# Routing's one-hot columns: GpSimd multiplies by the token codes, VectorE only compares

## The reference

```
x = x + 0.5 * ffn(layernorm(x))
x = x + attention(layernorm(x))     # 16 heads of 16, causal, 4096 x 4096 scores a head
x = x + 0.5 * ffn(layernorm(x))
```

```
vals, idx = top_k(softmax(x @ gate_w + gate_b, axis=tokens), 2)
y[e] = relu(relu(relu(x @ w1[e]) @ w2[e]) @ w3[e])          # with biases
v[e] = sum over tokens of y[e] * weight of the token for e
out  = sum over the token's two experts of v[e]
```

## Time and profile before

| | |
|---|---|
| median of 3 runs | 2114.99 us (2114.93 to 2117.0) |
| the profiled execution, its own time | 2126.23 us |
| its span | 2124.5 us |
| busy: TensorE / VectorE / ScalarE / GpSimd | 2047.7 / 1817.7 / 1598.6 / 414.5 us |
| mean granted TensorE clock | 0.975 |

### The profile page before, as it was taken

How to read it: one execution, slowest core, us unless ns; L and a number is a source line. 1 busy time by engine, 2 the same in 40 slices (tenths; PEclk the granted TensorE clock), 3 DMA queues, 4 the chain that set the end, 5 groups by cost and what they waited for, 6 DMA issues and landing times.

```text
span 2124.5 us, 99858 instructions
## 1 busy us (share of the span) xinstructions
PE 2047.7 (96%) x43659; PEld 1584.0 (75%) x43659; DVE 1817.7 (86%) x4023; ACT 1598.6 (75%) x3311; POOL 414.5 (20%) x1118
## 2 busy tenths in 40 slices
PE   5899989999999999999999999999999999879998
PEld 3788866377877777777787777777778776658885
DVE  6666666899999999999999999999999994676665
ACT  5344446599999999999999999999999998334442
POOL 1333213411121111121111111111111111023330
PEclk8899989999999999999999999999999999979998
DMA  8211103300010000100001001000010002231112
GB/s 273 74 47 50 42 16 125 134 30 25 13 34 14 25 30 8 34 20 18 31 7 33 22 16 34 9 29 27 11 34 16 22 4 69 54 118 47 45 49 88
DMA packets 70394, 94.36 MB, mean 44 GB/s; under 512 B 16640, under 2 KB 59396, under 8 KB 69956
## 3 DMA queue, kind: packets, MB, share of 16 engines
q1 hardware_dynamic: 62796, 68.75, 10.1%
q0 software_dynamic: 6816, 19.20, 3.4%
q10 hardware_dynamic: 344, 0.01, 0.0%
HBM read 62.24 MB, written 25.43 MB: 41 GB/s over the span
## 4 chain that ended last, share of the span: by engine, by line
PE 88%; DVE 6%; issue 2%; ACT 1%; POOL 1%; DMA 1%; SPq 1%; another core or an unknown queue 0%; DVEq 0%; ACTq 0%; POOLq 0%
PE bank L1264 39%; PE bank L1257 22%; PE bank L1139 17%; PE bank L1346 3%; PE bank L1150 1%; PE bank L1375 1%; DVE stats L1405 1%; PE bank L1307 1%; PE bank L1157 1%; DVE rows L1427 1%; DVE x_res L1725 1%; SPq L698 0%; POOL work L591 0%; DVE work L1594 0%; PE bank L1217 0%
## 5 line engine op out<-in xcount | busy, mean ns | idle before, releaser
L966 ACT ACTIVATE feat<-bank 128x512 f32<-128x512 f32 (+3 forms) x2304 | 1263.2, 565 | 113.8 <-PE bank L1264 13.3
L1264 PE MATMUL bank<-work 96*32 96x512 bf16 (+2 forms) x15872 | 1206.4, 370 | 5.0 <-DVE work L1772 3.8
L1772 DVE TENSOR_REDUCE work<-bank 128x1 f32<-128x512 f32 (+1 forms) x1920 | 1178.9, 659 | 26.4 <-PE bank L1264 23.4
L1257 PE MATMUL bank<-feat,phase 128*17 128x128 f32 (+3 forms) x18432 | 879.2, 263 | 0.3 <-ACT feat L972 0.3
L1257 PEld LDWEIGHTS bank<-feat,phase 128*17 128x17 f32 x18432 | 588.4, 98 | 270.7 <-ACT feat L972 13.7
L1264 PEld LDWEIGHTS bank<-work 96*32 96x32 bf16 (+1 forms) x15872 | 472.6, 96 | 57.1 <-DVE work L1772 24.6
L1139 PE MATMUL bank<-work 128*128 128x256 f32 (+1 forms) x1872 | 398.4, 363 | 0.6 <-issue 0.2
L1139 PEld LDWEIGHTS bank<-work 128*128 128x128 f32 x1872 | 325.1, 192 | 37.1 <-issue 1.0
L625 POOL TENSOR_SCALAR_AFFINE_SELECT feat<-feat 128x128 f32<-128x128 f32 x512 | 145.1, 292 | 456.0 <-ACT feat L966 439.1
L1656 DVE COPY work<-phase 128x514 f32 x234 | 101.5, 436 | 124.1 <-ACT work L880 99.5
L578 POOL DMA_INDIRECT work<-token_table,row_no x142 | 138.1, 973 | 299.0 <-PE bank L1150 142.6
(11 more groups left out here) (201 smaller groups left out, 1371.9 us busy)
## 6 DMA issues: line engine op xcount, KB each, us to landing
phase<-in_w SPq DMA_DIRECT2D x12, 1024.0 KB, 12.0
work<-qk_parts SPq DMA_DIRECT2D x60, 192.0 KB
token_table<-rows SPq DMA_DIRECT2D x8, 1056.0 KB, 8.7
work<-work SPq DMA_DIRECT2D x512, 0.5 KB
qk_parts<-phase SPq DMA_DIRECT2D x20, 384.0 KB, 2.8
work<-qk_parts SPq DMA_DIRECT2D x60, 128.0 KB
qk_parts<-work SPq DMA_DIRECT2D x12, 384.0 KB, 2.8
x_res<-in_x SPq DMA_DIRECT2D x8, 512.0 KB
```

The lines of the kernel that those rows point to most:

```text
L966: eng.activation(p_ring[:, n % P_RING, lo:QB], s_bank("probs", n)[:, lo:QB], ACT.Exp, scale=HD ** -0.5).then_inc(sig.s_done, 1)
L1257: mm = eng.matmul(bank[ACC_BANK][GRID * g:GRID * g + VW, GRID * i0:P], v_aug[:, t, h, :], weights[:, i0:TPJ, g, :], start=(t == 0), stop=( ...
L1264: mm = eng.matmul(out[GRID * g:GRID * (g + 1), width], left[:, GRID * g:GRID * (g + 1)], right, start=start, stop=stop)
L1772: eng.tensor_reduce(maxima[:, h % 2, j, PLACE[i], at:at + 1], scores[:, 0:hi - lo], AX_X, ALU.max).then_inc(sig.a_done, 1)
```

## The change

The 64 pairs go in five batches, of 8, 8, 16, 16 and 16. VectorE only compares (two instructions a batch, ten in all in place of twelve). The multiplication by the codes is put at the end of GpSimd's `route`, one instruction a batch, behind a wait for that batch's `hi` comparison. A new semaphore `coded` counts the multiplications, and TensorE waits for it beside `hots`. The batches of 8 use one half of the 16 columns of buffer 0 each.

```diff
+HOT_BATCHES = ((0, 8), (8, 16), (16, 32), (32, 48), (48, 64))
...
@@ GpSimd, route(f), behind the second partition_all_reduce
+                after()
+                for batch, (n0, n1) in enumerate(HOT_BATCHES):
+                    b, at, i0 = n0 // HOTS, slice(n0 % HOTS, n0 % HOTS + n1 - n0), n0 % NT
+                    need.wait_ge(sig.hots[f], 2 * batch + 1)
+                    eng.tensor_tensor(hot_hi[b][:, :, at], hot_hi[b][:, :, at],
+                                      bc(code_bf[:, i0:i0 + n1 - n0], 1, [P, N_SUB, n1 - n0]),
+                                      ALU.mult).then_inc(sig.coded[f], 1)
@@ TensorE, route(f)
-                    need.wait_ge(sig.hots[f], 3 * (b // HOTS + 1))
+                    batch = sum(n1 <= b for _, n1 in HOT_BATCHES)
+                    need.wait_ge(sig.hots[f], 2 * (batch + 1))
+                    need.wait_ge(sig.coded[f], batch + 1)
@@ VectorE, route(f)
-                for b in range(TOP * NT // HOTS):
-                    c, i0 = divmod(b * HOTS, NT)
-                    LO, HI = [P, P, HOTS], [P, N_SUB, HOTS]
-                    eng.tensor_tensor(hot_hi[b], hi_wide, bc(hi[:, c, i0:i0 + HOTS], 1, HI),
+                for n0, n1 in HOT_BATCHES:
+                    b, at, (c, i0) = n0 // HOTS, slice(n0 % HOTS, n0 % HOTS + n1 - n0), divmod(n0, NT)
+                    LO, HI = [P, P, n1 - n0], [P, N_SUB, n1 - n0]
+                    eng.tensor_tensor(hot_hi[b][:, :, at], hi_wide[:, :, at], bc(hi[:, c, i0:i0 + n1 - n0], 1, HI),
                                       ALU.is_equal).then_inc(sig.hots[f], 1)
-                    eng.tensor_tensor(hot_lo[b], lo_wide, bc(lo[:, c, i0:i0 + HOTS], 1, LO),
+                    eng.tensor_tensor(hot_lo[b][:, :, at], lo_wide[:, :, at], bc(lo[:, c, i0:i0 + n1 - n0], 1, LO),
                                       ALU.is_equal).then_inc(sig.hots[f], 1)
-                    need.wait_ge(sig.hots[f], 3 * b + 1)
-                    eng.tensor_tensor(hot_hi[b], hot_hi[b], bc(code_bf[:, i0:i0 + HOTS], 1, HI),
-                                      ALU.mult).then_inc(sig.hots[f], 1)
```

More of the change, by code:

```diff
@@ L297, in __init__ @@
         self.table, self.widened, self.hots = many("table_stored", 2), many("widened", 2), many("hots", 2)
+        self.coded = many("hots_coded", 2)
         self.chosen_tr, self.chosen_copy = many("chosen_tr", 2), many("chosen_copied", 2)
```

## The result

| | before | changed |
|---|---|---|
| median of 6 runs each | 2115.24 us (2114.93 to 2117.0) | 2128.66 us (2125.46 to 2129.86) |
| ratio to the runs of before | | 1.006, 95% interval 1.0047 to 1.0073 |
| profiled execution, its own time / span | 2126.23 / 2124.5 us | 2129.86 / 2128.1 us |

The changed kernel is slower by 13.4 us (2128.66 - 2115.24), and the interval stands clear of the 0.2% that can be told. The forecast was 2129.0 us, 14.0 us more.

What follows compares the result with a forecast made beforehand. VectorE's one-hots were taken to bound both routings; comparisons 7.32 us plus GpSimd's multiplications 9.62 us, without overlap, end 7.02 us later a routing, 14.0 us in all on 2114.99: 2129.0 us, range 2119 to 2134 us (8 in 10).

Steps and rivals of the forecast that it cites:

- What bounds the place: Both routings: one-hots on VectorE are the chain, 9.92 us; a microsecond at the last multiplication counts once per routing.
- Whether the two run side by side: Routing one-hots: VectorE's comparisons and GpSimd's multiplications hold each other for whole instructions, so none overlap; this decides the sign.
- one-sided: Rival for the routings: only VectorE is held, GpSimd starts beside a running comparison; 6.4 us slower, 2121.4 us; chance 0.10.
- GpSimd's price: GpSimd's five multiplications a routing: 2.36 us for 16 pairs, 1.27 us for 8, 9.62 us in all.
- VectorE's price: VectorE's ten comparisons a routing, halves 0.36 and 0.60 us, full ones 0.66 and 1.14 us: 7.32 us.
- The sum: First comparison to last multiplication: 7.32 + 9.62 = 16.94 us, 7.02 us later a routing, 14.0 us in two.
- I take the two as equal: Turns between VectorE and GpSimd: 0.1 us allowed per semaphore hand-over, cancelled by held instructions ending sooner after release.
- Cover and clock: Behind the last multiplication: VectorE's small instructions (2.01 us) end before TensorE's matmuls (2.46 us); TensorE's clock stays 0.50.
- The signs to look for: Routing trace: some hi comparisons 2 us or more, ending 0.1 to 0.2 us behind a multiplication; bank 7 read near 72.0 us.

Runs made afterwards that it cites:

- e3_probe: Kernel before, with GpSimd tensor_tensor, memset and copy on a spare tile, results unused, run beside VectorE's one-hots; 2122.02 us.
- e7_psum: Changed kernel with the two compared digits kept in PSUM (float32) instead of SBUF (bf16), so a comparison reads one SBUF tensor; 2123.96 us (one execution).
- e1_serial: Changed kernel, but GpSimd's five multiplications wait until all ten comparisons are done; 2130.39 us median, ratio to the kernel before 1.0062.

## Why the prediction was right

- *What bounds the place.* Right. The one-hots are the chain in both routings, and 5.83 us at the last multiplication is 5.9 us at each reading of bank 7, counted from the routing's first comparison (70.75 - 52.47 = 18.28 us in place of 64.97 - 52.59 = 12.38).
- *Whether the two run side by side.* Right, and this was the step that the sign hung on. It rested on a likeness (two SBUF streams to the held line 1427). e3_probe and e7_psum show the cause itself: GpSimd's memset doesn't hold a one-hot instruction, its copy and tensor_tensor do, and a comparison with one SBUF stream isn't held. The holding goes both ways: GpSimd's multiplication waited out the running comparison, so it wasn't one-sided.
- *GpSimd's price.* Near: 9.62 us for five was forecast, and undisturbed they print 1.13, 1.13, 2.33, 2.35 and 2.34 us, 9.28 in all (first routing of e7_psum). The extrapolation to 1136 elements held (2.36 us forecast); the half ones came out 0.14 us under their 1.27. The bf16 inputs and the runs of 8 or 16 brought no extra cost that shows. The 2.6 cycles an element of the Trainium skill (GPSIMD Engine Reference, section Elementwise — side-by-side cycle accounting) gave the prediction 10.7 us, an estimate from that page. That figure has 0.17 us an instruction added from the rows; 2.17 ns for each of the 4544 elements alone are 9.86 us, and the 9.28 us of this case stand below that too.
- *VectorE's price.* Right: the ten comparisons by themselves took 59.14 - 51.81 = 7.33 us in e1_serial, 7.32 forecast.
- *The sum.* Its size was off: 16.94 us forecast, 15.75 us measured. The term that was mis-sized is chiefly "I take the two as equal" of the hand-overs. An instruction that has waited on its engine is over sooner after its release than one that starts fresh, so each turn is shorter than its forecast: a full multiplication took 2.19 us for 2.36 (three times), a half one 1.00 for 1.27 (53.09 + 1.44 less the end of the lo comparison, 52.84 + 0.69; twice), a held hi comparison 0.06 less (four times). That is 3 x 0.17 + 2 x 0.27 + 4 x 0.06 = 1.3 us, against 1.2 us missing (16.94 - 15.75). 0.34 us of it is GpSimd's price (3 x 0.02 + 2 x 0.14, from the item above), the rest the hand-overs. Forecast 14.0 us, measured 11.7 in the two routings, and bank 7 was read at 70.75 us, not near 72.0.
- *That the time still came out at 2128.7 against 2129.0* is therefore partly luck: 11.7 us from the routings and 1.4 us (of 13.1 in the spans) to 1.7 us (of 13.4 in the medians) more that no row ties to the change. The 36 later runs of the kernel before have a median of 2117.4 us, 2.1 above the six beside the changed kernel; against them its 2128.66 us are 11.3 us more, which is what the routings alone give. They weren't timed beside it, so this is a hint and no proof that the 13.4 us are a little too much.
- *Cover and clock.* Right. VectorE's small instructions ended at 69.61 + 0.48 = 70.09 us, 0.66 us ahead of the reading. TensorE's granted clock was 0.50 (1.2 GHz) until 72 us, 0.54 from 72 to 74 us and 1.00 (2.4 GHz) from there; the first gather was issued at 71.53 us.
- *The signs to look for.* One was wrong in its detail: held hi comparisons end 0.60 us behind the multiplication, not 0.1 to 0.2. The 0.16 us of line 1427 didn't carry over to a longer instruction: in e1_serial the held cast of 39 elements was over 0.04 us behind the multiplication, line 1621 (312 elements) 0.33 us.

## What to carry to other kernels

Idle time on GpSimd is not free time for VectorE's work. While GpSimd's copies and tensor_tensors ran here, VectorE's casts and its instructions with two SBUF inputs stood still, so such a move costs the sum of both engines' times and not the longer of the two. Before moving elementwise work there, ask what VectorE has to do meanwhile; if that reads two SBUF streams and is the chain, leave it, or move a part of it to ScalarE, whose instructions ran beside VectorE's unhindered here (that took 0.9 us off a routing by the rows, too little for the times to tell). And in a trace, an instruction far longer than its like, which ends a fixed time behind another engine's instruction, is waiting and not working: subtract before calling an engine slow.

## What was not expected of the hardware

- A turn is cheaper than an instruction alone (2.19 against 2.34 us on GpSimd, 0.60 against 0.66 on VectorE), which fits a start-up that passes during the wait; no run takes that apart.
- GpSimd's copy of 1136 bf16 took about 1.0 us of its own (from the end of the lo comparison, 59.32 + 1.21, to 59.46 + 2.06), as its memset did with 1.04, and under half of its tensor_tensor's 2.34.
- The memset that left the comparisons alone held a cast of VectorE's, 1.13 us in place of 0.18 (e3_probe, second routing).
- One profiled execution of an unchanged kernel can lie 11 us (0.5%) above its runs and 9.5 us above another profiled one, most of that in the two tiles stages; two traces of before were needed to lay the difference out.
